# Graph attention and a hyperbolic graph layer: late tables loaded in the turns, node rows in blocks of 128

## The chip, the cores and the metric

The kernel runs on one core of a Trainium2 chip. The metric is the device time of one execution in microseconds, the median over a few executions. Before the change it is 957.39 us (three runs, 954.81 to 961.11).

## The reference, cut to what matters

There are 3125 nodes of 128 features and 53125 edges, sorted by target (`dst`). Two residual layers follow each other.

```
h = relu(layernorm(x));  Q, K, V = h@Wq+bq, h@Wk+bk, h@Wv+bv        # 8 heads of 16
score = sum(Q[dst]*K[src]) / 4 + edge_attr@We + be
p = softmax of score over the edges with the same dst
x2 = x + segment_sum(p * V[src], dst) @ Wo + bo

h = relu(layernorm(x2));  t = arctanh(clip(|h|)) / |h| * h
m = t @ W.T + b;  deg = degree of a node as source + as target;  dinv = deg ** -0.5
z = segment_sum(m[src] * dinv[src] * dinv[dst], dst)
out = x2 + tanh(|z|) / |z| * z
```

## The kernel before, in words

The edges are cut into 32 groups of 1664 (13 tiles of 128). As they are sorted by target, the targets of a group fit in a window of 128 nodes, whose first node is `base_of(g)`.

**The preparation** normalises the nodes, computes Q, K and V, and stores them in DRAM (`q_tab`, `kv_tab`, L543 to L554). DVE checks on the way that the graph is as the fast path needs it (`structure`, L880 to L945, result in `orderly_i`); each engine reads that word and takes the fast path or a slow one, edge tile by edge tile.

**The first layer** is a loop over the groups on all engines. Per group Pool gathers 13 tiles of K and V rows (`gather`, L758 to L768), and `keep_step` makes it wait for TensorE's steps, from group 2 on. SP works in turns: `turn(g)` (L633) loads the broadcast of the local targets of group g+1 (`dloc_b`, L571), the edge features of group g (`attr_s`, L578 and L580) and the Q window (`qwin`, L585), then waits for the finished rows of group g-2 (`s_x2`), stores them in `x2_tab` (L600) and loads the x window (L592). SP's transfers are in one queue, in order. TensorE multiplies the first chunk of group g+1's queries (L1736) towards the end of step g, so `qwin` of g+1 must be there by then. `stay_busy` (L1723) issues matmuls that compute nothing, to keep TensorE's clock up. DVE runs the chain of a group: products with K (L1043), sums per head (L1049), scans for the segment maxima, weights, sums, and in `settle` (L1163) the new rows of group g-2. The turns, steps and gathers of the early and late groups are written out, the rest are loops of two.

**The late tables** are the odd groups' source and target indices in two other layouts, which only the second layer needs. SP stores them flat in DRAM (`late_src`, `late_dst`, L612, in pieces of 52 bytes) right after the preparation, and reads them back in `load_late` (L602) before turn 2: two loads in pieces of 44 bytes (L606) and four in pieces of 4 bytes (L609). Each of the eight is cut into 2048 pieces (128 by 16). DVE derives what it needs in `late_rows` (L1305) between its steps 1 and 2.

**The middle** lies between the layers. SP stores the last rows of `x2_tab`, waits until all have landed, and loads the table back in five parts of five rows a partition (`xt`, L680). Node p*25+n lies in partition p, as `node_rows` has it. DVE takes mean and variance of each part (L1377 to L1382) and the squared norms (`square_norm`, L1168); ACT and TensorE normalise, transpose and multiply with W. DVE then computes `dinv_t` and the arctanh factors on 25 numbers a partition; one of them comes through a logarithm on ACT, which ACT does after `B1_FIRST` of its 25 bias rows (L1615 to L1618). DVE scales the rows (`hs_t`, L1424), SP stores them in `hs_tab` in five parts (L686), and when these have landed Pool begins the gathers of the second layer (`gather1`, L796). The count of outgoing edges `od_s` goes through DRAM to become `od_t`, 25 numbers a partition (L648, L650).

**The second layer** works on pairs of groups: even groups by counts in matrices (L1439, L1440, L1878, L1895), odd groups by gathered rows (L805, L1906). Its DVE part begins with `run_one_hots`.

Of the kernel before, what the change touches and what calls it, by code (L numbers as in the profile page):

```python
# [48 lines left out]
B1_FIRST = 9  # L49
# [68 lines left out]
ROUND = 12582912.0  # L118
SC = H + C + 1
# [22 lines left out]
def build(nc, x, src_t, dst_t, dst_before, dst_after, dst_first, dst_run, src_run, attr, wqkv, bqkv, we, be, wo, bo, w1t, b1,  # L142
# [14 lines left out]
    with ExitStack() as ctx:  # L157
# [50 lines left out]
        od_s = sb("od_s", [HI, LO])  # L208
# [46 lines left out]
        x2 = sb("x2", [P, 2, D + 1])  # L255

# [43 lines left out]
        src_hi = runs(place(late, 0))  # L300
# [20 lines left out]
        checks = S[:, 0].rearrange("p t e -> p (t e)")[:, 0:2 * GROUPS * T + GROUPS + 2 + 3 * DG * T]  # L321
        faults = sb("faults", [P, 1])
        faults_row = sb("faults_row", [1, P])
# [38 lines left out]
        s_od_st = sem("s_od_st")  # L362
# [131 lines left out]

        qkv_banks = [ps_q[0], ps_q[1], ps_r, ps_c]
# [24 lines left out]
        def _(sp):  # L520
# [81 lines left out]
            def load_late():  # L602

                sp.wait_ge(s_flat, 32)
                for rest, more, flat in ((src_rest, src_more, late_src), (dst_rest, dst_more, late_dst)):
                    sp.dma_start(rest[:], flat[:, MORE * P:].rearrange("n (p t) -> p n t", t=T2)).then_inc(s_more, 16)  # L606
                    with nc.allow_non_contiguous_dma("one edge to a partition"):
                        for k in range(MORE):
                            sp.dma_start(more[:, :, k], flat[:, P * k:P * (k + 1)].rearrange("n p -> p n")).then_inc(s_more, 16)  # L609

            for flat, edges in ((late_src, src_i), (late_dst, dst_i)):
                sp.dma_start(flat.rearrange("n (p t) -> p n t", t=T), edges[:, 1::2, :]).then_inc(s_flat, 16)  # L612
            in_order = orderly(sp, (s_base, 1))
            with sp.If_eq(in_order, 1):
# [16 lines left out]
                load_late()  # L631
# [1353 lines left out]
```

## Time and profile before

| What | Value |
|---|---|
| median of three runs | 957.39 us |
| the profiled execution: its own time, its span | 959.84 us, 957.4 us |
| mean granted TensorE clock | 0.956 |
| busy: PE, DVE, Pool, ACT | 798.9, 725.0, 604.5, 390.1 us |
| shares of the chain that ended last | PE 38%, issue 14%, DMA 14%, Pool 13%, DVE 12%, SP's queue 7% |
| preparation and opening, first query matmul | 63.4 us |
| steps of the first layer | 63 to 647 us |
| middle, until Pool's first gather of layer two | 647 to 686 us |
| second layer | 686 to 957 us |

Busy times overlap: they are what an engine executes, waits not counted. The chain is followed back from the last instruction, each time to what released it; "issue" is time in which an engine waited for nothing that the profile shows. A time such as 70.90 is always counted from the start of the span. A transfer's time to landing counts from its issue to its completion.

### The profile page before, as it was taken

The page shows a single profiled execution, that of the slowest core. Times are in us where ns is not written, and L with a number is a line of the kernel's source. Part 1 is how long each engine was busy: PE and PEld are TensorE (multiplying, and loading weights), DVE is VectorE, ACT ScalarE, POOL GpSimd, SP SyncE. Part 2 cuts the span into 40 slices and gives each one's busy share as a digit, 9 for nine tenths or more (in the row PEclk, how much of TensorE's full clock was granted, in tenths as well). Part 3 has the DMA queues.
Part 4 walks back from the last instruction along what each step waited for, and adds up shares of the span by engine and source line. Part 5 has one row for each costly group of instructions (what it writes and reads, how often), then busy time and mean ns, then how long its engine had stood idle before and what let it go on. Part 6 is the DMA issues. An engine that isn't in the chain of part 4 may idle for free.

```text
span 957.4 us, 21173 instructions
## 1 busy us (share of the span) xinstructions
PE 798.9 (83%) x5412; PEld 620.8 (65%) x5460; DVE 725.0 (76%) x2575; ACT 390.1 (41%) x1069; POOL 604.5 (63%) x597
## 2 busy tenths in 40 slices
PE   5538998999888988998998998975399989898983
PEld 2226676676676676676676676664187778777773
DVE  8826877787777777787777787758989788878752
ACT  3542324324324323333333333304945546555540
POOL 0175777777777777777777777700266666766662
PEclk9858999999999999999999999997699999999997
DMA  5795445445445445445545545402212222222221
GB/s 168 187 202 109 132 133 159 135 128 162 133 132 156 130 133 147 150 126 147 147 132 138 159 128 145 129 21 73 95 50 65 67 58 58 66 61 62 62 61 30
DMA packets 103351, 109.53 MB, mean 114 GB/s; under 512 B 36803, under 2 KB 81807, under 8 KB 103311
## 3 DMA queue, kind: packets, MB, share of 16 engines
q0 software_dynamic: 25600, 66.10, 26.3%
q1 hardware_dynamic: 77719, 43.07, 16.8%
q8 instruction: 12, 0.20, 0.1%
q14 instruction: 20, 0.16, 0.1%
HBM read 97.94 MB, written 11.16 MB: 114 GB/s over the span
## 4 chain that ended last, share of the span: by engine, by line
PE 38%; issue 14%; DMA 14%; POOL 13%; DVE 12%; SPq 7%; DVEq 1%; ACT 1%; POOLq 0%
POOL kv L805 13%; PE ps_s L1723 10%; PE ps_q L1736 10%; DMA qwin<-q_tab 7%; DMA kv<-hs_tab,idx 4%; PE ps_c L1715 3%; PE ps_f L1782 3%; DVE sc L1049 2%; PE ps_r L1895 2%; SPq L564 2%; PE ps_f L1806 1%; PE ps_f L1805 1%; PE ps_f L1906 1%; PE ps_c L1711 1%; PE ps_r L1755 1%
## 5 line engine op out<-in xcount | busy, mean ns | idle before, releaser
L766 POOL DMA_INDIRECT kv<-kv_tab,idx x416 | 434.1, 1044 | 188.2 <-issue 126.2
L805 POOL DMA_INDIRECT kv<-hs_tab,idx x176 | 170.0, 966 | 149.2 <-DMA hs_tab<-qkv 62.9
L1539 ACT ACTIVATE S<-iota,nloc 128x128 f32<-128x128 f32 x384 | 122.1, 389 | 233.4 <-PE ps_r L1755 233.1
L1723 PE MATMUL ps_s<-rep_hi,iota_b 128*128 128x512 bf16 x616 | 159.5, 384 | 7.7 <-issue 7.7
L1736 PE MATMUL ps_q<-qwin,ST 128*128 128x128 f32 x832 | 116.9, 286 | 12.7 <-DMA qwin<-q_tab 11.8
L1736 PEld LDWEIGHTS ps_q<-qwin,ST 128*128 128x128 f32 x832 | 105.2, 195 | 20.2 <-issue 13.5
L1755 PE MATMUL ps_r<-wv,S 128*128 128x137 f32 x832 | 109.3, 282 | 0.0
L1755 PEld LDWEIGHTS ps_r<-wv,S 128*128 128x128 f32 x832 | 103.4, 192 | 0.0
L1043 DVE TENSOR_TENSOR prod<-kv,ps_q 128x512 f32<-128x512 f32 (+1 forms) x128 | 73.5, 575 | 30.9 <-PE ps_q L1736 30.4
L1723 PEld LDWEIGHTS ps_s<-rep_hi,iota_b 128*128 128x128 bf16 x664 | 57.8, 98 | 54.0 <-issue 7.5
L1895 PE MATMUL ps_r<-qkv,xt 128*128 128x128 f32 x800 | 92.0, 275 | 0.8 <-ACT xt L1641 0.8
L1895 PEld LDWEIGHTS ps_r<-qkv,xt 128*128 128x128 f32 x800 | 90.6, 192 | 1.1 <-issue 1.1
L1630 ACT ACTIVATE S<-iota,rest_nloc 128x128 f32<-128x128 f32 x176 | 56.3, 388 | 53.3 <-PE ps_f L1887 53.3
L1049 DVE TENSOR_REDUCE sc<-prod 128x32 f32<-128x512 f32 (+1 forms) x128 | 70.9, 573 | 0.0
L1906 PE MATMUL ps_f<-kv,S 128*128 128x128 f32 x352 | 47.0, 294 | 27.4 <-DMA kv<-hs_tab,idx 27.4
L1439 DVE TENSOR_SCALAR ST<-bwd_reset 128x800 bf16<-128x800 f16 x128 | 56.5, 442 | 17.0 <-PE ps_q L1878 17.0
L1906 PEld LDWEIGHTS ps_f<-kv,S 128*128 128x128 f32 x352 | 44.3, 207 | 31.2 <-issue 20.4
L1127 DVE TENSOR_TENSOR wv<-kv,wv 128x1024 f32<-128x1024 f32 x64 | 62.5, 1018 | 0.5 <-ACT wv L1558 0.5
L1542 ACT ACTIVATE S<-S 128x512 f32<-128x512 f32 x96 | 60.5, 630 | 3.0
L1440 DVE TENSOR_SCALAR wv<-iota_b,bwd_reset 128x128 bf16<-128x128 bf16 x240 | 61.3, 255 | 0.0
L1715 PE MATMUL ps_c<-we,attr_s 128*128 128x32 f32 (+1 forms) x256 | 40.8, 269 | 19.4 <-DMA attr_s<-in_attr 19.4
L1782 PE MATMUL ps_f<-oh_lo,oh_hi 128*50 128x64 bf16 x416 | 56.7, 302 | 0.0
(265 smaller groups left out, 1223.8 us busy)
## 6 DMA issues: line engine op xcount, KB each, us to landing
dloc_b<-dloc_tab SPq DMA_DIRECT2D x32, 416.0 KB, 5.0
kv<-kv_tab,idx POOLq DMA_INDIRECT x416, 3.2
attr_s<-in_attr SPq DMA_DIRECT2D x32, 192.0 KB, 4.2
kv<-hs_tab,idx POOLq DMA_INDIRECT x176
kv_tab<-qkv SPq DMA_DIRECT2D x4, 640.0 KB, 3.4
x_tab<-x SPq DMA_DIRECT2D x32, 64.5 KB, 2.5
qwin<-q_tab SPq DMA_DIRECT2D x32, 64.0 KB, 3.9
xwin<-in_x SPq DMA_DIRECT2D x32, 64.0 KB
```

The lines of the kernel that those rows point to most:

```text
L766: pool.indirect_dma_start(out=kv[:, b, t, :], out_offset=None, in_=kv_tab, in_offset=bass.IndirectOffsetOnAxis(ap=idx[:, b, t:t + 1], axis ...
L805: pool.indirect_dma_start(out=kv[:, j, t, 0:D], out_offset=None, in_=hs_tab, in_offset=bass.IndirectOffsetOnAxis(ap=idx[:, j, t:t + 1], ax ...
L1043: V.tensor_tensor(prod[:, c % 2, 0:w, :], kv[:, b, t0:t1, 0:D], ps_q[c % 2][:, 0:w * D].rearrange("p (t d) -> p t d", d=D), ALU.mult).then ...
L1049: st.mark(V.tensor_reduce(sc[:, :, t0:t1].rearrange("p h t -> p t h"), prod[:, c % 2, 0:t1 - t0, :].rearrange("p t (h d) -> p t h d", d=DH ...
L1539: A.activation(S[:, b, t, :], iota[:], ACT.Abs, bias=nloc[:, g, t:t + 1] if known(g) else nloc[:, bass.ds(g, 1), t:t + 1].rearrange("p g t ...
L1715: mm = M.matmul(p_bias[:, 4 * H * k:4 * H * k + w], attr_s[0:r, b, k, :], we4[0:r, 0:w], start=False, stop=k == 3)
L1723: M.matmul(ps_s[1][:], iota_b[:], busy_cols, start=True, stop=True)
L1736: mm = M.matmul(ps_q[c % 2][:, (t - t0) * D:(t - t0 + 1) * D], ST[:, b, t, :], qwin[:, b, :], start=True, stop=True)
L1755: mm = M.matmul(ps_r[:, 0:C + 1], S[:, b, t, :], wv[:, t, :], start=(t == 0), stop=(t == T - 1))
L1782: mm = M.matmul(ps_f[0:HI, 3 * D:3 * D + LO], oh_hi[:, b, :, t], oh_lo[:, b, :, t], start=(t == 0), stop=(t == T - 1))
L1895: M.matmul(sums[0], counts[:, i, :], hs_t[:, i, :], start=(i == 0), stop=False)
L1906: M.matmul(sums[1], S[:, j, t, :], kv[:, j, t, 0:D], start=(t == 0), stop=False)
```

## The change

Four things are changed.

**The late tables.** The two flat stores and the six loads no longer stand before turn 0 and turn 2. Turns 2 to 11 are written out, and one transfer stands between two turns: the stores before turns 4 and 5, the six loads before turns 6 to 11. DVE's `late_rows` moves from before step 2 to before step 31.

**Pool's checks.** `keep_step` now holds for group 1 too.

**Node blocks of 128.** Node n*128+p now lies in partition p (`node_blocks`). The loads of `xt` and the stores of `hs_tab` so move rows one by one. A check is added that group 27 begins at node 2560 or later; then the first four parts (twenty blocks) of `x2_tab` are complete once group 26 is stored, and SP loads them after turn 31, before the last two stores. Only the last part is loaded after all rows have landed. The statistics of part 0 and the source places are computed by DVE around its last step. `od_t` is made by two matmuls in place of the way through DRAM, and `dinv_tab` is written from a transposed copy.

**Order in the middle.** `B1_FIRST` goes from 9 to 6; the copies of the first gather indices (`set_rest`) go from before the statistics to before the wait for the logarithm; the seven instructions that make `iota_key` go from before the statistics to after the last `hs_t` row.

```diff
-B1_FIRST = 9
+B1_FIRST = 6
...
+SOON = NT // PCH - 1
+SOON_NODES = SOON * PCH * P
+LATE_GROUP = GROUPS - 5
...
-        od_s = sb("od_s", [HI, LO])
+        od_wide = sb("od_wide", [HI, 3 * LO])
+        od_s = od_wide[:, LO:2 * LO]
+        dinv_rows = agT[0:NT, :]
...
+        def node_blocks(tab):
+
+            return tab.rearrange("(n p) d -> p n d", p=P)
...
-            def load_late():
-                sp.wait_ge(s_flat, 32)
-                for rest, more, flat in ((src_rest, src_more, late_src), (dst_rest, dst_more, late_dst)):
-                    sp.dma_start(rest[:], flat[:, MORE * P:].rearrange("n (p t) -> p n t", t=T2)).then_inc(s_more, 16)
-                    with nc.allow_non_contiguous_dma("one edge to a partition"):
-                        for k in range(MORE):
-                            sp.dma_start(more[:, :, k], flat[:, P * k:P * (k + 1)].rearrange("n p -> p n")).then_inc(s_more, 16)
-            for flat, edges in ((late_src, src_i), (late_dst, dst_i)):
+            def load_blocks(c):
+                rows = slice(PCH * c, PCH * c + PCH)
+                sp.dma_start(xt[:, rows, :], node_blocks(x2_tab)[:, rows, :]).then_inc(s_x2l[c], 16)
+            def store_flat(flat, edges):
                 sp.dma_start(flat.rearrange("n (p t) -> p n t", t=T), edges[:, 1::2, :]).then_inc(s_flat, 16)
+            def load_rest(rest, flat):
+                sp.dma_start(rest[:], flat[:, MORE * P:].rearrange("n (p t) -> p n t", t=T2)).then_inc(s_more, 16)
+            def load_more(more, flat, k):
+                with nc.allow_non_contiguous_dma("one edge to a partition"):
+                    sp.dma_start(more[:, :, k], flat[:, P * k:P * (k + 1)].rearrange("n p -> p n")).then_inc(s_more, 16)
...
-                load_late()
...
-                with sp.Fori(1, GROUPS // 2 - 1) as n:
+                turn(2, 0)
+                turn(3, 1)
+                store_flat(late_src, src_i)
+                turn(4, 0)
+                store_flat(late_dst, dst_i)
+                turn(5, 1)
+                sp.wait_ge(s_flat, 32)
+                load_rest(src_rest, late_src)
+                turn(6, 0)
+                load_rest(dst_rest, late_dst)
+                turn(7, 1)
+                load_more(src_more, late_src, 0)
+                turn(8, 0)
+                load_more(dst_more, late_dst, 0)
+                turn(9, 1)
+                load_more(src_more, late_src, 1)
+                turn(10, 0)
+                load_more(dst_more, late_dst, 1)
+                turn(11, 1)
+                assert MORE == 2
+                with sp.Fori(6, GROUPS // 2 - 1) as n:
                     turn(2 * n, 0)
                     turn(2 * n + 1, 1)
                 turn(GROUPS - 2, 0)
                 turn(GROUPS - 1, 1, more=False)
+                sp.wait_ge(s_x2st, 16 * LATE_GROUP)
+                for c in range(SOON):
+                    load_blocks(c)
                 store_nodes(GROUPS - 2, 0)
-                sp.wait_ge(s_od, GROUPS)
-                sp.dma_start(od_tab.rearrange("(h l) o -> h (l o)", l=LO), od_s[:]).then_inc(s_od_st, 16)
-                sp.wait_ge(s_od_st, 16)
-                sp.dma_start(od_t[:], od_tab.rearrange("(p n) o -> p (n o)", n=NT)).then_inc(s_odl, 16)
                 store_nodes(GROUPS - 1, 1)
                 sp.wait_ge(s_x2st, 16 * GROUPS)
...
-            for c in range(NT // PCH):
-                rows = slice(PCH * c, PCH * c + PCH)
-                sp.dma_start(xt[:, rows, :], node_rows(x2_tab)[:, rows, :]).then_inc(s_x2l[c], 16)
-            sp.wait_ge(s_dinv, 1)
-            sp.dma_start(dinv_tab.rearrange("(p n) o -> p (n o)", n=NT), dinv_t[:]).then_inc(s_dvst, 16)
+                    sp.dma_start(od_t[:], od_tab.rearrange("(n p) o -> p (n o)", p=P)).then_inc(s_odl, 16)
+                for c in range(SOON):
+                    load_blocks(c)
+
+            load_blocks(SOON)
+            sp.wait_ge(s_dvrow, 1)
+            sp.dma_start(dinv_tab.rearrange("(n p) o -> n (p o)", p=P), dinv_rows).then_inc(s_dvst, 16)
             for c in range(NT // PCH):
                 rows = slice(PCH * c, PCH * c + PCH)
                 sp.wait_ge(s_hs, PCH * (c + 1))
-                sp.dma_start(node_rows(hs_tab)[:, rows, :], hs_t[:, rows, :]).then_inc(s_hsst, 16)
+                sp.dma_start(node_blocks(hs_tab)[:, rows, :], hs_t[:, rows, :]).then_inc(s_hsst, 16)
...
-                        if not (known(g) and g < 2):
+                        if not (known(g) and g == 0):
                             keep_step(g, t)
...
+                    pre.mark(V.tensor_scalar(checks[:, c3 + GROUPS + 2:c4], base_f[:, LATE_GROUP:LATE_GROUP + 1],
+                                             float(SOON_NODES), None, ALU.is_lt))
...
+            def source_places(M_):
...
+            def row_stats(M_, c):
+                tiles = range(PCH * c, PCH * c + PCH)
+                dve.wait_ge(s_x2l[c], 16)
+                for i in tiles:
+                    M_.mark(V.bn_stats(st6[:, i, :], xt[:, i, 0:D]))
+                M_.sync()
+                for i in tiles:
+                    M_.mark(V.bn_aggr(mv[:, i, :], st6[:, i, :]))
+                M_.sync()
+                V.tensor_scalar(neg_mean[:, PCH * c:PCH * c + PCH], mv[:, PCH * c:PCH * c + PCH, 0], -1.0, None, ALU.mult)\
+                    .then_inc(s_mean2, 1)
             in_order = orderly(dve, (s_tab[0], 16))
             with dve.If_eq(in_order, 1):
+                M_ = Steps(nc, dve, s_dM, 0)
                 row_one_hots(0, 0)
                 step(0, 0, nodes=False, old=False)
                 step(1, 1, old=False)
-                late_rows()
                 step(2, 0)
                 step(3, 1)
                 with dve.Fori(2, GROUPS // 2 - 1) as n:
                     step(2 * n, 0)
                     step(2 * n + 1, 1)
                 step(GROUPS - 2, 0, far=False)
+                late_rows()
                 step(GROUPS - 1, 1, more=False, far=False)
+                source_places(M_)
                 step(GROUPS, 0, edges=False)
+                row_stats(M_, 0)
                 new_rows(GROUPS - 1, 1)
+                dve.wait_ge(s_odT, 1)
+                M_.mark(V.tensor_copy(od_t[:], ps_s[0][:, 0:NT]))
...
-            for j in range(2):
-                set_rest(j, j)
...
-            for k in range(0, NT * W, P):
-                w = min(P, NT * W - k)
-                M_.mark(V.tensor_scalar(iota_key[:, k:k + w], iota[:, 0:w], float(k), None, ALU.add))
-            M_.sync()
...
+            for c in range(1, NT // PCH):
+                row_stats(M_, c)
+                for i in range(PCH * (c - 1), PCH * c):
                     square_norm(i)
-            dve.wait_ge(s_odl, 16)
...
+            for j in range(2):
+                set_rest(j, j)
             dve.wait_ge(s_ln, 1)
...
             V.memset(R[:, 1, :], 0.0).then_inc(s_R1, 1)
+            for k in range(0, NT * W, P):
+                w = min(P, NT * W - k)
+                M_.mark(V.tensor_scalar(iota_key[:, k:k + w], iota[:, 0:w], float(k), None, ALU.add))
+            M_.sync()
             dve.wait_ge(s_hs, NT)
...
                     A.activation(lnv[:], rat[:], ACT.Ln, bias=1.0).then_inc(s_ln, 1)
+                    act.wait_ge(s_dinvT, 1)
+                    A.copy(dinv_rows, ps_f[0:NT, 0:P]).then_inc(s_dvrow, 1)
...
+                pe.wait_ge(s_od, GROUPS)
+                M.matmul(ps_s[0][:, 0:NT], od_wide[:, LO:3 * LO], ident[0:HI, 0:HI:2], start=True, stop=False)
+                M.matmul(ps_s[0][:, 0:NT], od_wide[:, 0:2 * LO], ident[0:HI, 1:HI:2], start=False, stop=True).then_inc(s_odT, 1)
+                pe.wait_ge(s_x2, 2 * GROUPS)
...
+            pe.wait_ge(s_dinv, 1)
+            M.transpose(ps_f[0:NT, 0:P], dinv_t[:], ident[:]).then_inc(s_dinvT, 1)
+            pe.wait_ge(s_dvrow, 1)
```

## Rows read from the trace of the kernel before

**Rows 1.** SP's issues in the opening (start us, us, engine, line, transfer, count).

```profile
41.62 3.22 SPq L612 DMA_DIRECT2D late_dst<-dst_i  x1
50.92 1.08 SPq L580 DMA_DIRECT2D attr_s<-in_attr  x1
```

**Rows 2.** Transfers: size, then us from issue to landing; the attr_s issued at 50.92.

```profile
late_dst<-dst_i SPq DMA_DIRECT2D x1, 104.0 KB, 12.1
attr_s<-in_attr SPq DMA_DIRECT2D x1, 16.0 KB, 10.5
kv<-kv_tab,idx POOLq DMA_INDIRECT x416, 3.2
```

**Rows 3.** DMA packets in the stretches 41:46, 46:50 and 74:78 us.

```profile
DMA packets 3042, 0.79 MB, mean 158 GB/s; under 512 B 2116, under 2 KB 3026, under 8 KB 3041
...
DMA packets 2029, 0.35 MB, mean 87 GB/s; under 512 B 1969, under 2 KB 1969, under 8 KB 2029
...
DMA packets 4944, 0.47 MB, mean 118 GB/s; under 512 B 4841, under 2 KB 4841, under 8 KB 4944
```

**Rows 4.** Pool's last gathers of groups 0 and 1, in order of time.

```profile
58.95 0.95 POOL L766 DMA_INDIRECT kv<-kv_tab,idx  x1 [0.30 <-issue]
...
75.92 0.94 POOL L766 DMA_INDIRECT kv<-kv_tab,idx  x1 [0.30 <-DVE idx L842]
```

**Rows 5.** DVE's last product of groups 0 and 1.

```profile
70.90 0.29 DVE L1043 TENSOR_TENSOR prod<-kv,ps_q 128x128 f32<-128x128 f32 x1
...
88.58 0.29 DVE L1043 TENSOR_TENSOR prod<-kv,ps_q 128x128 f32<-128x128 f32 x1
```

**Rows 6.** SP between turns, before an even turn and before an odd one.

```profile
126.07 0.34 SPq L592 DMA_DIRECT2D xwin<-in_x  x1
127.03 0.34 SPq L571 DMA_DIRECT2D dloc_b<-dloc_tab  x1
...
144.19 0.34 SPq L592 DMA_DIRECT2D xwin<-in_x  x1
144.77 0.33 SPq L571 DMA_DIRECT2D dloc_b<-dloc_tab  x1
```

**Rows 7.** TensorE's query matmuls of an even group, and all such waits (us, times, longest).

```profile
133.70 1.15 PE L1736 MATMUL ps_q<-qwin,ST 128*128 128x128 f32 x8 [0.65 <-DMA qwin<-q_tab]
...
PE ps_q L1736 <- DMA qwin<-q_tab: 11.8, 15, 1.5
```

**Rows 8.** The same 22 matmuls after a short and after a longer wait.

```profile
767.44 2.72 PE L1906 MATMUL ps_f<-kv,S 128*128 128x128 f32 x22 [1.51 <-DMA kv<-hs_tab,idx]
...
784.26 4.32 PE L1906 MATMUL ps_f<-kv,S 128*128 128x128 f32 x22 [2.43 <-DMA kv<-hs_tab,idx]
```

**Rows 9.** Engines in 632:636 us (busy PE, PEld, DVE, ACT, POOL; clock; DMA share; GB/s).

```profile
632.00:636.00 4.00, 3.22 (x20) 1.96 (x19) 1.97 (x8) 0.20 (x1) 0.00 (x0) 1.00 0.00 0
```

**Rows 10.** DVE around its last step and in the middle, in order of time.

```profile
643.82 0.17 DVE L1133 TENSOR_SCALAR fb<-ps_c 128x8 f32<-128x8 f32 x1 [4.31 <-PE ps_c L1763]
...
647.16 0.29 DVE L1160 TENSOR_TENSOR x<-ps_f,xwin 128x128 f32<-128x128 f32 x1 [1.68 <-PE ps_f L1806]
...
653.28 1.07 DVE L1377 BATCH_NORM_STATS2 st<-xt 128x6 f32<-128x128 f32 x5 [2.37 <-DMA xt<-x_tab]
...
675.40 0.19 DVE L1415 SCALAR_TENSOR_TENSOR sm<-lnv,sm 128x25 f32<-128x25 f32 x1 [1.51 <-ACT lnv L1618]
```

**Rows 11.** The chain of waits in the middle: the last part's statistics.

```profile
663.17 0.99 DVE st L1377 x5
```

**Rows 12.** ACT's bias rows ahead of the logarithm.

```profile
671.03 2.74 ACT L1615 ACTIVATE ST<-b_s,dinv_t 128x128 f32<-128x128 f32 x9 [2.79 <-DVE dinv_t L1395]
```

**Rows 13.** Stores in rows of 512 bytes: size, us to landing.

```profile
q_tab<-qkv SPq DMA_DIRECT2D x5, 320.0 KB, 4.1
```

**Rows 14.** Pool's first gather of layer two, and TensorE's waits for gathered rows there.

```profile
686.05 0.94 POOL L805 DMA_INDIRECT kv<-hs_tab,idx  x1 [62.90 <-DMA hs_tab<-qkv]
...
PE ps_f L1906 <- DMA kv<-hs_tab,idx: 27.4, 14, 7.0
```

More of the change, by code:

```diff
@@ L299, in build @@
         late = bwd_reset8[:].rearrange("p g h t -> p (g h t)")
-        src_hi = runs(place(late, 0))
+        src_lane = runs(place(late, 0))
         src_key = runs(place(late, 1))
@@ L658, in _ @@
                 sp.wait_ge(s_partrow, 2)
-                load_late()
+                store_flat(late_src, src_i)
+                store_flat(late_dst, dst_i)
+                sp.wait_ge(s_flat, 32)
+                for rest, more, flat in ((src_rest, src_more, late_src), (dst_rest, dst_more, late_dst)):
+                    load_rest(rest, flat)
+                    for k in range(MORE):
+                        load_more(more, flat, k)
                 sp.wait_ge(s_e_blank, 3)
@@ L675, in _ @@
                     wait_apart(sp, s_n_put, 16 * n + 16, (s_base, 1))
-                sp.dma_start(od_t[:], od_tab.rearrange("(p n) o -> p (n o)", n=NT)).then_inc(s_odl, 16)
-            for c in range(NT // PCH):
-                rows = slice(PCH * c, PCH * c + PCH)
-                sp.dma_start(xt[:, rows, :], node_rows(x2_tab)[:, rows, :]).then_inc(s_x2l[c], 16)
-            sp.wait_ge(s_dinv, 1)
-            sp.dma_start(dinv_tab.rearrange("(p n) o -> p (n o)", n=NT), dinv_t[:]).then_inc(s_dvst, 16)
+                with nc.allow_non_contiguous_dma("one node to a partition"):
+                    sp.dma_start(od_t[:], od_tab.rearrange("(n p) o -> p (n o)", p=P)).then_inc(s_odl, 16)
[4 more added lines that the diff above has]
+            sp.dma_start(dinv_tab.rearrange("(n p) o -> n (p o)", p=P), dinv_rows).then_inc(s_dvst, 16)
             for c in range(NT // PCH):
@@ L877, in _ @@
             c0, c1_, c2_, c3 = 0, GROUPS * (T - 1), GROUPS * T, 2 * GROUPS * T
-            c4, c5, c6 = [c3 + GROUPS + 2 + k * DG * T for k in range(3)]
+            c4, c5, c6 = [c3 + GROUPS + 3 + k * DG * T for k in range(3)]
             far_off = checks[:, c6:].rearrange("p (g t) -> p g t", g=DG)
@@ L1345, in _ @@
                     node_tile(n)
-            def set_rest(n, j):
-                V.tensor_copy(idx[:, j, 0:T2], src_rest[:, n, :] if known(n) else
-                              src_rest[:, bass.ds(n, 1), :].rearrange("p g t -> p (g t)")).then_inc(s_idx1, 1)
-            M_ = Steps(nc, dve, s_dM, 0)
-            for j in range(2):
-                set_rest(j, j)
-            M_.mark(V.tensor_scalar(src_hi[:, :, 0:T], src_run_i[:], -(NT // 2), 1.0 / NT, ALU.add, ALU.mult))
-            M_.then(V.tensor_scalar(src_hi[:, :, T:], src_more[:], -(NT // 2), 1.0 / NT, ALU.add, ALU.mult))
@@ L1359, in _ @@
-            M_.then(V.tensor_scalar(src_hi, src_hi, ROUND, None, ALU.add))
-            M_.then(V.tensor_scalar(src_hi, src_hi, ROUND, None, ALU.subtract))
-            M_.mark(V.scalar_tensor_tensor(out=src_key[:, :, 0:T], in0=src_hi[:, :, 0:T], scalar=-float(NT), in1=src_run_i[:],
-                                           op0=ALU.mult, op1=ALU.add))
-            M_.then(V.scalar_tensor_tensor(out=src_key[:, :, T:], in0=src_hi[:, :, T:], scalar=-float(NT), in1=src_more[:],
-                                           op0=ALU.mult, op1=ALU.add))
@@ L1365, in _ @@
[L1365 to L1384 removed]
+                dve.wait_ge(s_odl, 16)
@@ L1385, in _ @@
+                M_ = Steps(nc, dve, s_dM, 0)
+                source_places(M_)
+                row_stats(M_, 0)
+                M_.mark(V.tensor_copy(od_t[:], od_t[:]))
+            for c in range(1, NT // PCH):
+                row_stats(M_, c)
+                for i in range(PCH * (c - 1), PCH * c):
                     square_norm(i)
-            dve.wait_ge(s_odl, 16)
             M_.mark(V.tensor_scalar(v3[:, 0, :], mv[:, :, 1], EPS_LN, None, ALU.add))
```

43 lines of the change are left out of this document (22 added, 21 removed).

## The prediction

> **What bounds the kernel now.** I read the chain of waits first. It has three regimes: an opening in which TensorE waits for transfers, 31 steps in which TensorE, DVE and SP's queue hand work to each other, and a second layer that runs at Pool's pace. The middle between the layers is one chain on DVE. The change touches the opening, the turns of eight steps, and the middle.
>
> Opening: SP's timeline shows the edge features of group 0 issued at 50.92 us and 10.5 us to landing [rows 1, 2]. TensorE's first work needs them. The packet counts say why: from 41 to 50 us the 16 DMA engines worked off 2116 + 1969 packets below 512 bytes [rows 3]. These are the two flat stores of the late tables, 2048 pieces each. All that SP issued behind them waited.
>
> Steps: TensorE waited in 15 of 32 steps for the Q window, 11.8 us together; the row of one step shows 0.65 us [rows 7]. So the window lands just when TensorE comes to it, and what delays SP's queue between two turns delays the step. That is the reading on which this forecast rests.
>
> Middle: after the last new rows (647.16) they are stored, the table is loaded, and DVE begins the statistics at 653.28; the last part begins at 663.17 [rows 10, 11]. Pool starts at 686.05, when `hs_tab` has landed [rows 14].
>
> **The opening.** Removed from SP's queue are two stores before turn 0 and six loads before turn 2. The second store alone held SP for 3.22 us [rows 1], and its landing took 12.1 us [rows 2]. Without them the features are issued some 4 us sooner and no longer wait behind 4096 small packets. The next bound is Pool: its 13th gather of group 0 is issued at 58.95 [rows 4], which does not move, and lands 3.2 us later [rows 2], at 62.15. DVE's last product of group 0 was at 70.90 [rows 5]. That gives 62.15 - 70.90 = **-8.75 us**. Group 1: Pool's last gather is issued at 75.92 and lands at 79.1; the product would be at 88.58 - 8.75 = 79.8 [rows 4, 5], so Pool just keeps up. Bounds: -3.8 (only SP's own time is won, half a microsecond and 3.22) and -10 (the last gather lands faster in emptier queues).
>
> Pool's checks for group 1 make it wait for TensorE's steps of group 0. By TensorE's order these come ahead of group 1's products, and Pool is 13 gathers long over group 0 first; I take 0, at most +1 with 79.1 against 79.8. `late_rows`, four short DVE instructions, leaves one step and enters another: 0.
>
> **The turns.** Between turns 3 and 11 stand eight transfers of 2048 pieces, each on SP's queue straight ahead of the broadcast, the features and the Q window of the next group, issued only when SP has been released by `s_x2`. DVE and TensorE do not wait for them, but the Q window behind them comes later. How long does one occupy the engines? In 74:78 us, 4841 small packets went in 4 us [rows 3], with Pool's gathers beside them: 2048 / (4841 / 4) = 1.69 us for a load. The two stores: 4085 packets in at most 9 us; the table stores issued ahead of them ran for perhaps 2.5 of it (an estimate), so 6.5 / 2 = 3.25 us each. Bounds for a store: 1.69 as for a load, and (41.62 + 12.1 - 41.0) / 2 = 6.3 us from its landing [rows 1, 2].
>
> What hides them: turns 2 to 11 are now written out. The step from the x window's issue to the broadcast's was 0.96 us before an even turn, with the loop's branch, and 0.58 before an odd one [rows 6], so an even turn wins 0.38. Odd steps did not wait for the window; their slack is between 0 and 0.65, and I take 0.3. An even load costs 1.69 - 0.38 = 1.31, an odd one 1.39: three of each, 8.1 us. The stores: 3.25 - 0.38 = 2.87 and 2.95, together 5.8 us. Turn 2 wins its 0.4. I find no slack behind the Q window: the filler matmuls, the queries and the products stand in order, and a step that waited 0.65 was longer by about as much.
>
> Waits of 3 us may lower TensorE's granted clock. The rows show it: the same 22 matmuls took 2.72 us after a wait of 1.51, and 4.32 us after one of 2.43, when the granted clock had fallen from 2.4 to 1.2 GHz [rows 8]. One such fall costs 1.6 us; I count one. Sum: 8.1 + 5.8 - 0.4 + 1.6 = **+15.1 us**.
>
> The Trainium skill would make this term smaller. Its page "DMA: Bandwidth & Descriptors", section "Measured (HBM→SBUF, 128 partitions, SWDGE, issued from GpSimd)", gives about 10.5 ns per packet and engine, hence 1.34 us for 128 packets on each of 16 engines, load or store. By that estimate the turns would cost 9.2 us and the time would be 950.3. This trace shows 13.2 ns (4 us times 16 over 4841), and its time is used.
>
> **The middle.** Twenty blocks are loaded before the last two stores; the DMA share in 632:636 is 0.00 [rows 9], so they are hidden, if that cover holds. The statistics of part 0 (1.07 for five [rows 10] and about 0.6 for the rest) go into DVE's wait of 1.68 before the last new rows, the source places into its wait of 4.31 [rows 10]: 0. After the last new rows, at about 647.5, comes the copy of `od_t`, then parts 1 to 3 with the norms of parts 0 to 2. These took 663.17 - 653.28 = 9.89 less part 0's 1.66, so 8.2. Part 4 then begins at 648.0 + 8.2 = 656.2 in place of 663.17 [rows 11]: **-6.95 us**. Its rows, stored and loaded as part 0's were, are there at about 653.3, 2.9 us before they are wanted. `B1_FIRST`: three bias rows of 2.74 / 9 [rows 12] leave the way to the logarithm, **-0.9 us**, as DVE waited 1.51 for it [rows 10]; what remains, 0.6, covers the two copies of `set_rest`.
>
> `hs_tab` is now stored in rows of 512 bytes. The nearest row is `q_tab`, 4.1 us to landing behind a store twice its size [rows 13]; between 0 and 2, I take **+0.3**. Seven `iota_key` instructions, 1 us, go behind the last `hs_t` row: TensorE's counts start later, Pool's gathers do not. TensorE waits there 27.4 / 14 = 2 us a pair for gathered rows [rows 14], so the 1 us is made up: 0. The transposed `dinv_tab` and the two matmuls for `od_t` stand beside longer work: 0. Sum of the middle: **-7.55 us**, bounds -4 and -8.5.
>
> **The sum.** -8.75 + 15.1 - 7.55 = -1.2. The profiled execution (959.84, span 957.4) would be 958.6, span 956.2. It lies 2.45 over the median of the runs, so the median goes from 957.39 to **956.2 us**.
>
> **Rivals.** About 1% (9.6 us, so below 947.8 or above 967.0) is what a measurement can tell from no change.
>
> (a) The small transfers sink into gaps of the steps. For it: the DMA engines have idle stretches in every step, and 4 or 44 bytes a piece move almost no data. Against it: they sit where the queue is fullest. Turns at +1, the time is 942. Faster by over 1% needs turns of at most +6.7. Chance 0.22.
>
> (b) Slower: the waits of the Q window pull TensorE's clock down in each of the eight steps (8 x 1.6 = 12.8), and a store costs its upper bound (5.9 + 6.0). With the loads 8.1 - 0.4 + 12.8 + 11.9 = 32.4 us, the time is 973.5. It decides from turns of +25.9. For it: rows 8, and that a wait of 2.43 was enough. Against it: filler matmuls surround the wait. Chance 0.20.
>
> (c) The opening wins only SP's 3.8 us, since broadcasts and gathers crowd the queues anyway: 961.1. Chance 0.10.
>
> (d) The change does not do what it says: the new check fails and the slow path is taken, far above any range. Group 27 begins at edge 44928 of 53125, near node 2643 if targets are even, above 2560. Chance 0.01.
>
> **The numbers.** The forecast has 0.47, its own range 945 to 968; of it 0.10 lie below 947.8 and 0.02 above 967. Faster: 0.22 + 0.10 = 0.32; slower: 0.20 + 0.02 + 0.01 = 0.23; the rest, 0.45, within 1%. The range from 942 to 968 leaves out about half of (a) and most of (b).
>
> **What would show it.** Opening: DVE's last product of group 0 near 62, and Pool without a pause up to group 2. Turns: TensorE's waits for the Q window of 1 to 3 us in the steps that prepare groups 4 to 11, and these steps 1.3 to 3 us longer than the 17.7 of the step from group 0 to 1 [rows 5]. Middle: last part's statistics 8.7 us after the last new rows, before 15.7; Pool's first gather 31 us after them, before 38.6. I am wrong if those eight steps are as long as the others, if TensorE's clock falls in more than two of them, or if the first product of the opening still waits for features.

## The result, and the profile after

| | before | after |
|---|---|---|
| device time, median of 5 runs each (us) | 957.18 (954.51 to 961.11) | 966.92 (963.58 to 969.85) |
| ratio, 95% interval | | 1.0104 (1.0064 to 1.0144) |
| profiled execution, its span (us) | 959.84, 957.4 | 969.01, 967.0 |
| mean granted clock of TensorE | 0.956 | 0.949 |

The change is 1% slower. The forecast was 956.2 us, 1.2 below the kernel before; 966.92 still lies in its range of 945 to 968, but on the other side of the kernel before. The steps can be followed by DVE's last product of each group. Before, that of group 0 is at 70.90 us, of group 3 at 124.5, of group 11 at 267.8, of group 31 at 627.12. After, DVE's timeline has, for groups 0, 3, 4 and 5:

```profile
62.25 0.29 DVE L1087 TENSOR_TENSOR prod<-kv,ps_q 128x128 f32<-128x128 f32 x1
...
116.00 0.27 DVE L1087 TENSOR_TENSOR prod<-kv,ps_q 128x128 f32<-128x128 f32 x1
144.15 0.27 DVE L1087 TENSOR_TENSOR prod<-kv,ps_q 128x128 f32<-128x128 f32 x1
168.79 0.27 DVE L1087 TENSOR_TENSOR prod<-kv,ps_q 128x128 f32<-128x128 f32 x1
```

So 8.65 us are won at group 0 and 8.5 are left at group 3. Then the step of group 4 takes 28.15 us and that of group 5 24.64, where it was 18.1 and 17.6. At group 11 (282.2) the kernel is 14.4 us behind, at group 31 (640.12) 13.0. Eight steps lost 22.9 us, 17.1 of it in the two that follow the stores.

SP's timeline from the new rows of group 1 on, with the store of `late_src` in it (start, us, line, transfer):

```profile
116.16 0.36 SPq L611 DMA_DIRECT2D x_tab<-x  x1
117.32 0.35 SPq L603 DMA_DIRECT2D xwin<-in_x  x1
117.71 0.43 SPq L620 DMA_DIRECT2D late_src<-src_i  x1
118.24 2.13 SPq L582 DMA_DIRECT2D dloc_b<-dloc_tab  x1
120.46 0.39 SPq L589 DMA_DIRECT2D attr_s<-in_attr  x1
120.89 0.48 SPq L591 DMA_DIRECT2D attr_s<-in_attr  x1
122.17 0.35 SPq L596 DMA_DIRECT2D qwin<-q_tab  x1
```

The store itself costs SP 0.43 us. The broadcast behind it takes 2.13 to issue, where it took 0.34 [rows 6]; behind the seven other late transfers it took 1.74 to 2.74. And the window behind them is long in flight. The chain of waits, after then before (start, us, what):

```profile
122.17 7.14 DMA qwin<-q_tab
129.31 0.22 issue
129.53 2.07 PE ps_q L1794 x8
131.60 1.71 PE ps_s L1781 x4
```

```profile
129.57 3.91 DMA qwin<-q_tab
133.70 1.15 PE ps_q L1736 x8
134.85 0.86 PE ps_s L1723 x4
```

TensorE waited 4.96 us, then ran at half its rate. Its rows in this step, and the windows view (busy PE, PEld, DVE, ACT, POOL; granted clock; DMA share; GB/s):

```profile
124.34 0.22 PE L1848 MATMUL ps_b<-ident,c 8*128 8x8 f32 x1
129.53 2.07 PE L1794 MATMUL ps_q<-qwin,ST 128*128 128x128 f32 x8 [4.96 <-DMA qwin<-q_tab]
...
140.90 1.75 PE L1794 MATMUL ps_q<-qwin,ST 128*128 128x128 f32 x10
142.49 2.75 PE L1813 MATMUL ps_r<-wv,S 128*128 128x137 f32 x22
```

```profile
110.00:129.00 19.00, 13.56 (x92) 10.31 (x91) 15.02 (x46) 5.63 (x16) 14.12 (x14) 0.98 0.73 138
129.00:142.00 13.00, 12.47 (x45) 9.40 (x46) 2.97 (x4) 2.07 (x6) 4.62 (x4) 0.50 0.19 59
...
157.00:162.00 5.00, 4.31 (x15) 2.88 (x15) 1.82 (x3) 0.28 (x2) 1.48 (x1) 0.50 0.18 61
```

In the second stretch nothing is late any more but TensorE itself: granted 1.2 GHz (0.50), 96% busy, DMA engines at 0.19. The granted clock is 0.50 from 128.3 to 141.8 us. The third stretch lies behind the wait of 4.89 us in the step of group 5; there it is 0.50 only from 155.6 to 162.3 us. These are the only two falls in the steps. A wait of 2.49 us in the step of group 9 is followed by none (granted clock 1.00 in 236:244). Over the kernel its waits for the window grew from 11.8 us [rows 7] to

```profile
PE ps_q L1794 <- DMA qwin<-q_tab: 25.3, 19, 5.0
```

The middle: from the last product (640.12) to Pool's first gather, 54.3 us after and 58.9 before.

```profile
651.97 5.81 PE L1813 MATMUL ps_r<-wv,S 128*128 128x137 f32 x26
...
662.21 0.62 PE L1885 MATMUL ps_s<-ident,od_wide 50*128 50x25 f32 x2
662.66 0.60 PE L1886 MATMUL ps_s<-ident,od_wide 50*128 50x25 f32 x2
```

```profile
650.00:656.00 6.00, 5.64 (x23) 5.23 (x24) 4.32 (x14) 0.27 (x1) 0.00 (x0) 0.54 0.04 11
```

```profile
662.32 0.29 DVE L1204 TENSOR_TENSOR x<-ps_f,xwin 128x128 f32<-128x128 f32 x1 [0.63 <-PE ps_f L1864]
663.30 0.18 DVE L1412 COPY od_t<-ps_s 128x25 f32<-128x25 f32 x1 [0.63 <-PE ps_s L1886]
663.91 1.07 DVE L1385 BATCH_NORM_STATS2 st<-xt 128x6 f32<-128x128 f32 x5 [0.43 <-issue]
...
672.07 1.11 DVE L1385 BATCH_NORM_STATS2 st<-xt 128x6 f32<-128x128 f32 x5
```

```profile
694.42 0.94 POOL L847 DMA_INDIRECT kv<-hs_tab,idx  x1 [59.48 <-DMA hs_tab<-qkv]
```

The last part's statistics begin 9.75 us after the last new rows, before 16.0 [rows 10, 11]. The way from the last product to those new rows is longer: 22.2 us for 20.0, because the granted clock fell to 0.5 (0.54 in 650:656) and 26 window sums took 5.81 us for 4.48. The second layer takes what it took: from Pool's first gather to the end of the span 272.6 us, before 271.3.

### The profile page after: what moved, and what is told of

Its sections match the earlier page's. It is cut to its first block, busy times and chain, and to the rows that moved or that the text cites. A ratio compares the mean times of both kernels' runs of the same rounds, so it can differ in the third digit from the quotient of the medians.

```text
span 967.0 us, 21100 instructions
## 1 busy us (share of the span) xinstructions
PE 818.2 (85%) x5465; PEld 629.1 (65%) x5465; DVE 725.3 (75%) x2577; ACT 390.7 (40%) x1070; POOL 602.6 (62%) x597
## 4 chain that ended last, share of the span: by engine, by line
PE 35%; POOL 15%; DMA 15%; issue 14%; DVE 10%; SPq 9%; DVEq 1%; ACT 1%; POOLq 0%
POOL kv L847 15%; PE ps_s L1781 10%; PE ps_q L1794 10%; DMA qwin<-q_tab 8%; DMA kv<-hs_tab,idx 4%; PE ps_c L1773 3%; SPq L582 2%; PE ps_f L1840 2%; DVE sc L1093 2%; SPq L575 2%; PE ps_f L1864 1%; PE ps_f L1863 1%; PE ps_c L1769 1%; PE ps_r L1813 1%; SPq L589 1%
## 5 line engine op out<-in xcount | busy, mean ns | idle before, releaser
L1781 PE MATMUL ps_s<-rep_hi,iota_b 128*128 128x512 bf16 x664 | 174.7, 392 | 0.0
L1794 PE MATMUL ps_q<-qwin,ST 128*128 128x128 f32 x832 | 119.8, 291 | 25.8 <-DMA qwin<-q_tab 25.3
L1794 PEld LDWEIGHTS ps_q<-qwin,ST 128*128 128x128 f32 x832 | 108.3, 200 | 33.8 <-issue 27.9
L1495 DVE TENSOR_SCALAR ST<-bwd_reset 128x800 bf16<-128x800 f16 x128 | 56.2, 439 | 17.6 <-PE ps_q L1943 17.4
L1840 PEld LDWEIGHTS ps_f<-oh_lo,oh_hi 128*50 128x50 bf16 x416 | 48.9, 172 | 0.7
```

The lines of the kernel that those rows point to most:

```text
L1781: M.matmul(ps_s[1][:], iota_b[:], busy_cols, start=True, stop=True)
L1794: mm = M.matmul(ps_q[c % 2][:, (t - t0) * D:(t - t0 + 1) * D], ST[:, b, t, :], qwin[:, b, :], start=True, stop=True)
L1840: mm = M.matmul(ps_f[0:HI, 3 * D:3 * D + LO], oh_hi[:, b, :, t], oh_lo[:, b, :, t], start=(t == 0), stop=(t == T - 1))
```

## The experiments

**Theories.** By place in the queue, a late transfer costs because the window stands behind it on SP's queue. By shared engines, it costs wherever it stands. Beside them, the clock theory: most of the loss is not the wait but the 1.2 GHz behind it.

**How sharp the sums are.** The intervals of the undisturbed ratios are 0.2 to 0.4% to each side, 2 to 4 us, so a difference between two changed kernels is good to some 3 to 5 us. A median of few runs can also lie beside its ratio. So sums are given by medians and, where it matters, by ratios.

**A disturbed stretch.** In the first nine runs the kernel before took 1112 to 1130 us (medians), in the later nine, about an hour on, 956.4 to 956.8. The two stretches also ran on different chips, so no run tells whether the hour or the chip made the difference. In the first nine the steps took 17 to 27 us, most of them 20 to 23. A part of this comes from gaps in which TensorE waited for nothing that the profile shows; its waits in 90:610 us, of the unedited change (us, times, longest):

```profile
PE ps_b L1801 <- issue: 33.5, 20, 3.6
...
PE ps_q L1794 <- DMA qwin<-q_tab: 10.9, 6, 3.9
```

The ratios of that stretch are told, but the sums are made with the later nine.

**Tables as before.** Stores ahead of turn 0, loads ahead of turn 2.

```diff
+            for flat, edges in ((late_src, src_i), (late_dst, dst_i)):
+                store_flat(flat, edges)
             in_order = orderly(sp, (s_base, 1))
...
+                sp.wait_ge(s_flat, 32)
+                for rest, more, flat in ((src_rest, src_more, late_src), (dst_rest, dst_more, late_dst)):
+                    load_rest(rest, flat)
+                    for k in range(MORE):
+                        load_more(more, flat, k)
...
-                store_flat(late_src, src_i)
-                turn(4, 0)
...
```

> The changed kernel with its late tables written and read where the kernel before did: both stores ahead of turn 0, six loads ahead of turn 2. The middle and Pool's checks stay changed. What it tells: the share of the turns plus the opening against the share of the middle. If the traces are read rightly (opening -8.7 us, eight turns +22.9, middle -4.6, second layer about +1), it should run 957.2 - 4.6 + 1 = about 953.6, and DVE's last product of group 0 should be back near 70.9. Rival 1, the forecast's own middle (-7.55): 949.6. Rival 2, the middle brings nothing once the clock is no longer disturbed: 957.

> Late tables stored and read where the kernel before does it; middle and Pool's checks as changed. The kernel before runs at 956.4 us again. Trace theory: the middle brings 4.6 us: 951.8, ratio 0.995. Forecast's middle: -7.55, 948.9, ratio 0.992. Rival, the middle brings nothing: 1.000.

Disturbed: 0.980 (0.972 to 0.988) and 0.985 (0.970 to 1.000). Undisturbed: 947.78 of 956.55, ratio 0.991 (0.988 to 0.994). The middle brings 8.8 us. That is more than the 4.6 of the trace of after and a little more than the forecast's 7.55, within the interval. TensorE in the last step, and Pool's first gather of the second layer, 49.9 us after the last product:

```profile
635.36 3.22 PE L1799 MATMUL ps_r<-wv,S 128*128 128x137 f32 x26
```

```profile
674.00 1.03 POOL L833 DMA_INDIRECT kv<-hs_tab,idx  x1 [53.47 <-DMA hs_tab<-qkv]
```

In the kernel before, run as a kernel of its own on another chip, it is 58.8 us; up to the last product the two run level (624.1 and 624.5). The 26 window sums took 3.22 us at 2.4 GHz. This stretch depends on when the clock falls in it: over the undisturbed traces of the changed kernels it is 49.9 to 54.3 us, and no experiment holds the clock fixed there.

**All eight behind the window** of the same turn, where SP waits some 12 us for new rows.

```diff
-                def turn(g, b, more=True):
+                def turn(g, b, more=True, small=lambda: None):
...
                     load_edges(g, b)
+                    small()
                     store_nodes(g - 2, b)
...
-                turn(3, 1)
-                store_flat(late_src, src_i)
+                turn(3, 1, small=lambda: store_flat(late_src, src_i))
...
```

> The changed kernel with each of its eight late transfers moved by three places on SP's queue: behind the Q window of the same turn, where SP would wait about 12 us for the new rows anyway. Nothing else is moved. Theory 1, place in the queue: a late transfer costs because the window of the next group stands behind it; the eight turns then cost about +1 in place of +22.9 and the time is about 966.9 - 22 = 945. Theory 2, shared DMA engines: 2048 small pieces delay gathers and windows wherever they stand; the time stays above 960. Between them (about 953) both hold a half.

> All eight late transfers behind the Q window, a third time, beside the kernel before and its trace. If the chip is as in the first comparison: 945, ratio 0.987. If it is as in the runs since: ratio 0.98, DVE's last product of group 5 about 15 us ahead of that of the kernel before less what the steps scatter.

Disturbed: 0.978 (0.969 to 0.987) and 0.985 (0.969 to 1.000). Undisturbed: 941.81 of 956.42, ratio 0.988 (0.984 to 0.992). The steps of groups 4 and 5 are 17.75 and 17.60 us. Place in the queue holds; the eight transfers cost 966.9 - 941.8 = 25.1 us where the change puts them (by the ratios, 1.0104 - 0.9877 of 957, it is 21.7).

**Only the stores behind, only the loads behind.** The two mixed cases: one kind of transfer is moved, the other stays where the change puts it.

> Only the two stores behind the Q window, the six loads ahead of the broadcasts. All behind the window took 941.8. If the loads cost the 5.8 us of the trace, 947.6, ratio 0.991; if they cost the 8.1 us of the forecast, 950, ratio 0.993; if the stores were the whole of it, 942, ratio 0.985.

> Only the six loads behind the Q window of their turns; the two stores stay ahead of the broadcasts. If stores and loads cost independently, 941.8 + (966.9 - 953.4) = 955.3, ratio 0.999, with the steps of groups 4 and 5 at 28 and 25 us and those of 6 to 11 at 17.5 to 18.5. If the loads only cost because the stores had already thrown the order of the steps out, about 966.

Stores behind: 953.41, ratio 0.997 (0.995 to 0.999); in the disturbed stretch 0.971 (0.960 to 0.981). Loads behind: 959.29, ratio 1.002 (0.998 to 1.005), with steps 27.35 and 27.25 for groups 4 and 5 and 17.7 to 18.0 for 6 to 11. So with the loads out of the way the stores cost 17.5 us, and with the stores out of the way the loads 11.6: sum 29.1 for 25.1 together. My 955.3 was 4 us too low, but that is no more than the noise: by the ratios it is 13.2 and 8.5, sum 21.7, and 21.7 together. So the two kinds add up as far as these runs can tell. The loads' mechanism is another one. The chain of waits of after, at the first load:

```profile
170.50 0.43 SPq L624
170.92 0.05 issue
171.02 2.19 SPq L582
...
175.39 2.94 DMA qwin<-q_tab
```

The window is not longer in flight, it is issued 2 us later, because SP sits 2.19 us in the next broadcast's issue.

**Filler ahead of the two long waits.** The wait stays; TensorE works in it.

```diff
+                    if known(g) and g in (3, 4):
+                        stay_busy(20)
                     query(g + 1, 1 - b, (0,))
...
```

TensorE's steps 2 to 5 are also written out for it, in place of its loop.

> The changed kernel with 20 more filler matmuls (about 4.3 us by 1.03 for 4 or 5) on TensorE ahead of its two waits of 4.9 us for the Q windows of groups 4 and 5; four steps of its loop are written out for that. The wait stays, only what TensorE does in it changes. If the clock fall is a cost of its own beside the wait, as the trace reads (1.2 GHz granted for some 12 us after the first wait, 5 us after the second), the two steps come to about 23 and 22 us in place of 28.2 and 24.6, and the time falls by 5 to 7 us to about 961. Rival: the slow clock hides behind DVE, and the steps stay as long: 967.

> The changed kernel with 20 filler matmuls (4.5 us) ahead of TensorE's waits for the windows of groups 4 and 5. Clock theory: the waits stay about as long but the clock stays at 2.4 GHz, which took 5.5 us from each of the two steps in the earlier run; the steps come to about 23 and 20 us in place of 28.2 and 24.6 and the time to 957, ratio 1.000. If the wait alone costs, 1.010 as the unedited change.

Disturbed: 0.989 (0.981 to 0.996), steps 21.7 and 21.8 where the unedited change had 27.2 and 27.2. Undisturbed: 957.23, ratio 1.002 (0.999 to 1.005). TensorE in the step of group 4:

```profile
124.55 4.49 PE L1781 MATMUL ps_s<-rep_hi,iota_b 128*128 128x512 bf16 x20
128.88 1.05 PE L1794 MATMUL ps_q<-qwin,ST 128*128 128x128 f32 x8
...
134.93 1.28 PE L1794 MATMUL ps_q<-qwin,ST 128*128 128x128 f32 x10
136.04 2.75 PE L1813 MATMUL ps_r<-wv,S 128*128 128x137 f32 x22
```

```profile
129.00:142.00 13.00, 11.71 (x84) 9.63 (x84) 8.09 (x21) 3.26 (x10) 8.40 (x8) 1.00 0.42 94
```

The query matmuls now start when the filler ends, 12.8 us after the last product of group 3 in place of 13.5. No wait for the window is left, so this trace doesn't show when it landed, only that it was there by then. From their start to the end of the last query matmul it is 7.3 us in place of 13.1 in this step, and 7.3 in place of 9.6 in the next, so the lower clock cost 5.8 + 2.3 = 8.1 us. The rest of what the two steps lose (21.64 and 21.73 for 28.15 and 24.64, 9.4 us) is the earlier start. Writing the steps out is not the cause: groups 2 and 3, written out without filler, took 17.43 and 18.00 us for 17.43 and 17.40. The clock theory holds for a part: of the 25.1 us, 966.9 - 957.2 = 9.7 go with the filler (8.1 by the ratios), most of it the clock. That most of the loss is the clock is not so.

**Tables from inputs.** The host lays four more inputs out (slices and transposes); no stores, no small pieces.

```diff
+                for table, laid in ((src_rest, rest_src), (dst_rest, rest_dst), (src_more, more_src), (dst_more, more_dst)):
+                    sp.dma_start(table[:].rearrange("p g t -> p (g t)"), laid).then_inc(s_more, 16)
```

> No late tables in DRAM at all: the rest of each odd group and its two more columns come as four further inputs that the host lays out (slices and transposes), read by four transfers of 128 pieces ahead of turn 2. This is the price of all eight small-piece transfers together, opening included. By either theory the opening keeps -8.7 and the turns fall to 0: 966.9 - 22.9 = about 944, and a little more if the four loads delay group 2. If it is slower than e2, the four loads' place costs; if it is faster by several us, the small pieces of e2 still cost something where they stand.

> The kernel with the late tables read from inputs, with one more edit: six filler matmuls on TensorE ahead of the wait for agn in the last two steps, where the loop's own fifth filler is left out, and where the clock fell to 1.2 GHz in the trace (26 window sums in 5.81 us in place of some 3.3, node products 0.8 in place of 0.49). If the clock then stays at 2.4 GHz, the last new rows come about 20 us after the last product in place of 22.4, and the time is 2 to 3 us below the version without filler (ratio 0.968 if that one is at 0.971). Rival: the fillers stand in the way of the transposes and the gain is under 0.5 us.

Disturbed: 0.970 (0.962 to 0.977), and again 1081.23 of 1113.26. Undisturbed, with the filler of the next kernel: 944.96, ratio 0.988 (0.985 to 0.990). No faster than all eight behind the window: there the small pieces cost nothing that shows. Its turns 2 to 11 are in SP's loop again, which may be why it is not faster: its eight steps of groups 4 to 11 took 143.8 us, those of all eight behind the window 141.6, of the kernel before 143.3. The loop was not tried apart.

**Filler in the last two steps**, added to all eight behind the window.

```diff
                     if edges and more:
                         stay_busy(BUSY[4])
+                    elif known(g) and g >= GROUPS - 1:
+                        stay_busy(6)
```

> All eight transfers behind the Q window, and six filler matmuls ahead of the waits for agn in the last two steps. All behind the window alone took 941.8. If the clock then stays at 2.4 GHz to the end of the layer, 2 to 3 us less: 939 to 940, ratio 0.982. Rival: the clock falls there just the same or the fillers only fill, 941.8, ratio 0.985.

943.56, ratio 0.989 (0.986 to 0.991): no gain over 941.81. There was little to gain: the 26 window sums took 3.22 us, and 3.21 in the kernel without this filler, whose clock had not fallen there either. The profiled run has another loss, the step of group 3 with 21.5 us: the window issued just ahead of the store was late. With only the stores behind, the same step took 24.7 us (that profiled run, 960.6 us, is the slowest of its nine):

```profile
108.52 1.24 PE L1793 MATMUL ps_q<-qwin,ST 128*128 128x128 f32 x8 [2.52 <-DMA qwin<-q_tab]
109.56 1.91 PE L1780 MATMUL ps_s<-rep_hi,iota_b 128*128 128x512 bf16 x4
```

Its window was 7.0 us to landing, with the store issued 0.4 us behind it; the page's median for that kernel's windows is 3.9. In the two other traces with a store right behind this window it was 6.9 and 5.6 us. So the shared engines matter too. The Trainium skill, "DMA: Bandwidth & Descriptors", section "Queues, rings and completion order", says that an engine consumes descriptors in ring order, and that a later one may still finish its write before an earlier one. That leaves room for a transfer issued later to get in the way of the window, but gives no price; the price here is the 7.0 for 3.9.

**Issued when the window has landed**, added to that.

```diff
                     load_edges(g, b)
-                    small()
+                    if small:
+                        sp.wait_ge(s_qwin[b], 16 * ((g - b) // 2 + 1))
+                        small()
```

> The version with all eight behind the window and filler at the end, with one wait more: SP waits until the Q window of the turn has landed and only then issues the small transfer; it has some 12 us there before the new rows come. Theory: the step of group 3 then takes 17.4 to 18 us in place of 21.5, and the time is 939 to 941, ratio 0.983. Rival: the pieces now fall on Pool's gathers of the next group, whose products wait for them: 943.6 or more, ratio 0.9865.

939.26 of 956.78, ratio 0.9823 (0.9797 to 0.9849): the fastest, 17.5 us below before and 27.7 below the change (which was measured beside other runs of before). Its SP and DVE rows:

```profile
102.79 0.35 SPq L596 DMA_DIRECT2D qwin<-q_tab  x1
107.39 0.38 SPq L620 DMA_DIRECT2D late_src<-src_i  x1
116.54 0.35 SPq L611 DMA_DIRECT2D x_tab<-x  x1
117.69 0.35 SPq L603 DMA_DIRECT2D xwin<-in_x  x1
118.13 0.38 SPq L582 DMA_DIRECT2D dloc_b<-dloc_tab  x1
```

```profile
116.38 0.27 DVE L1082 TENSOR_TENSOR prod<-kv,ps_q 128x128 f32<-128x128 f32 x1
133.80 0.27 DVE L1082 TENSOR_TENSOR prod<-kv,ps_q 128x128 f32<-128x128 f32 x1
151.39 0.27 DVE L1082 TENSOR_TENSOR prod<-kv,ps_q 128x128 f32<-128x128 f32 x1
```

```profile
PE ps_q L1789 <- DMA qwin<-q_tab: 5.8, 8, 1.0
```

The store goes out 4.6 us behind the window, is landed (6.1 us) before the next turn, and the broadcast takes 0.38 again. Every step from group 2 to group 13 is 17.4 to 17.6 us, and TensorE has no wait for a window over 0.3 us before 336 us.

**The change again, and the kernel before itself.**

> The changed kernel once more, unedited, beside the kernel before. In the eight runs so far the kernel before took 1113 to 1130 us in place of 957, with gaps of 2 to 3 us between instructions that wait for nothing in the trace. If the chip is as in the first comparison, the ratio is 1.010 and the step of group 4 is 28 us. If it is as in the eight runs, the Q window no longer lands last in a step, so that what delays it is partly hidden: ratio 0.99, the step of group 4 about 25 us.

> The kernel before, unedited, to have its trace on the chip of these runs; the trace shown of before is of 957 us, and here it took 1112 to 1130. Ratio 1.000. The first opening, DVE's last product of group 0, should be at 70.9 as before (that part has no loops) and the steps about 21 us in place of 18. If Pool's first gather of the second layer comes 59 us after DVE's last product of the last group, as before, the middle is not touched by what makes the steps long; if it comes later, then the middle of this kernel pays for it as well, and the changed kernel's shorter middle is worth more here.

The unedited change in the disturbed stretch: ratio 0.988 (0.977 to 0.998), faster there than the kernel before. Its two steps after the stores took 27.2 us each, near the 28.15 and 24.64 undisturbed, with waits of 3.91 and 3.37 us. The gain must lie elsewhere, and there is no trace of before from that stretch. Why the sign turns stays open. The kernel before as a kernel of its own: 956.78 of 956.42, and 58.8 us from last product to Pool's first gather. Its first product came at 68.39, 2.5 us sooner than in the trace of before.

## Why the prediction was wrong

**Opening, -8.75: right in the trace.** The first product came at 62.25 for 62.15. Group 1 came at 81.17 for 79.8, Pool waited for nothing in it; the step of 18.9 us is there with the tables as before too, and its cause was not looked for. But the reading leans on one trace: in the second trace of the kernel before, group 0's product came at 68.39 and not at 70.90, and with tables as before at 69.69, while the seven undisturbed traces with the late transfers in the turns have it at 62.25 to 62.85. So the opening is worth 5.5 to 8.7 us, and that the forecast hit the upper end is luck. In medians it is 947.8 - 941.8 = 6.0, or 8.5 against the fastest kernel.

**Turns, +15.1: the step that failed.** Measured +22.9 in the trace.
- The loads, 8.1: the trace has 5.8 more in these six steps, the medians 11.6 without the stores (8.5 by the ratios). The forecast took the transfer's time on the engines. What it costs is SP's time in the broadcast behind it, 2.2 us, and at times a clock fall: with only the stores behind, the step of group 9 waited 1.69 us and took 23.9.
- The stores, 5.8 and one clock fall of 1.6, so 7.4: measured 17.1 in the trace, 17.5 in medians. With filler in the waits the two steps are still 7.6 us over those of before, near the 5.8.
- **The clock fall** is the term that was mis-sized. I took its price from 22 matmuls behind a wait [rows 8], 1.6 us; there the granted clock was 0.5 for only 3.4 us (784.7 to 788.1). After the first late window it was 0.5 for 13.5 us, over 7.3 us of work at full rate, all of it on the path, and cost 5.8; and it came a second time, for 6.7 us, and cost 2.3. Together that is 8.1 for 1.6. "Filler matmuls surround the wait" was the argument against; they stand ahead of it and behind it, not in it.

None of the three signs of being wrong that the forecast named came up: the eight steps were longer, the clock fell in two of them and not in more, and the opening no longer waited for features. But its sign for the turns, steps 1.3 to 3 us longer, missed the two after the stores, 10 and 7 us longer than in the trace of before. It counted falls, and the price was in how long they lasted.

Rival (b) was the right mechanism, given 0.20: windows late, the clock pulled down. It put a fall of 1.6 into each of eight steps, 12.8 in all. There were two, of 5.8 and 2.3. The stores were not at its upper bound.

**The Trainium skill's figure.** The forecast weighed 10.5 ns a packet (the Trainium skill, "DMA: Bandwidth & Descriptors", section "Measured (HBM→SBUF, 128 partitions, SWDGE, issued from GpSimd)"), with the time 950.3. The figure there is of loads; that it holds on each engine and for stores was my reading. The trace of after has a store of 2048 pieces 7.0 us in flight in the turns and a load 3.9 to 4.6, so stores are dearer than that reading allows. Why is open: both have pieces far below 512 bytes, and no run tried larger ones.

**Middle, -7.55: right in size, and hidden in the one trace.** It was 4.6 in the trace of after, and 8.8 in medians where the turns were as before, a little outside its bounds of -4 to -8.5. Its terms in the trace of after: part 4's statistics stood 9.5 us behind the end of the last new rows (662.6) for 8.7 forecast (the copy of `od_t` waited 0.63 for two matmuls that I had at 0, and 0.43 for issue). From the last row of `hs_t` to the gather it was 3.6 us, before 3.0, so +0.6 for +0.3. DVE's wait for the logarithm fell from 1.51 to 0.28, more than the 0.9. What came out better with the turns as before is the clock in the last step, where before itself lost about 1.3 us (window sums 4.48 for 3.22), and what was worse in after is the same clock (5.81).

**The sum as it came.** From group 0 to the end of the span: -8.65 + 0.15 + 22.9 (the eight turns) - 1.4 (the other steps) - 4.6 + 1.3 (second layer) = +9.7, in spans 967.0 - 957.4 = 9.6. The forecast erred by 7.8 in the turns and 3 in the middle. In the turns it is the clock behind two late windows, 8.1 for 1.6; beside it the stores came 3 dearer and the loads 2 cheaper. In the middle it is a clock fall in the last step, which no late window precedes; what brings it on there was not looked for.

## What to carry over

Before a transfer is put on a busy queue, ask what stands behind it and who waits for that; the same eight transfers cost 22 to 25 us ahead of the window and nothing that shows once it had landed, in a stretch where the queue's engine waited anyway. Price a clock fall by all the work at half rate that lies on the path until it ends, not by the next group of matmuls. And where a wait can't be removed, filler inside it is worth trying: 4.5 us of useless matmuls in each of two waits gave back 8 to 10 us.

## What the runs showed of the hardware

- After a wait of 4.96 us TensorE was granted 1.2 GHz for 13.5 us (8 query matmuls 2.07 us for 1.05 to 1.15), after one of 4.89 for 6.7 us, and after one of 2.52 and one of 1.69, in the run with only the stores behind, for some 10 us each (granted clock 0.50 in 109.6:119.6 and 225.6:235.6). After one of 2.49 it stayed at 2.4 GHz. With 20 filler matmuls in the two longest waits it stayed at 2.4 GHz.
- A DMA issue can hold its engine when many small pieces stand ahead of it: 1.74 to 2.74 us for the broadcast behind 2048 small pieces in the trace of after, 0.33 to 0.38 in the other steps, and 0.38 where the small pieces had landed first.
- A Q window was 7.14 us in flight behind such a store, 5.6 to 7.0 just ahead of one, 2.94 behind a load, 3.91 in the kernel before.
- For a stretch of time, and on other chips, the same program took 1112 to 1130 us in place of 957, with gaps of up to 3.6 us between instructions, and a comparison made in it had the other sign.
- Turns written out on SP: all steps of groups 2 to 13 took 17.4 to 17.6 us in the fastest kernel, while in its loop every second one took mostly 18.0 to 18.5. The rest of the loop written out was not tried.
